# The end of the 16-head attention: each mix of the last pair waits for its own chunk and writes its own PSUM bank, and the last chunk is inverted in two halves

## The reference

```python
x = x + jnp.tanh(g_xattn[0]) * _L0_xattn_ref(ctx_1024, mask_BxS2_bf1, _layernorm(x, axis=-1), ...)
x = x + jnp.tanh(g_ffn[0]) * _L0_ffn_ref(_layernorm(x, axis=-1), ...)
...
# in _L0_xattn_ref: HEADS = 16, DIM_HEAD = 64, 2048 queries, 1601 + 2048 keys
alphas = jax.nn.softmax(sim, axis=-1)
out = jnp.einsum('bhqf,bhfd->bhqd', alphas, v)
out = out.transpose(0, 2, 1, 3).reshape(b, q_len, INNER)
return out @ Wo
```

## Time and profile before

| | us |
|---|---|
| median of 3 runs | 3281.27 (3280.16 to 3281.69) |
| profiled execution, its own time | 3278.4 |
| its span, first to last instruction | 3276.5 |
| PE busy | 3067.5 |
| VectorE busy | 2211.0 |
| ScalarE busy | 1951.7 |
| last product with V to the last add (the part around the change) | 1800.1 to 1816.5 on the span |

### The profile page before, as it was taken

The page is one execution under the profiler, slowest core; times in us unless marked ns, Lnnn a source line. Parts: engine busy times, 40 slices in busy tenths (PEclk is TensorE's granted clock), DMA queues, the critical chain, the costliest instruction groups (busy, mean ns, idle before and its releaser), DMA issues. The chain is left out here.

```text
span 3276.5 us, 69950 instructions
## 1 busy us (share of the span) xinstructions
PE 3067.5 (94%) x29122; PEld 1640.0 (50%) x29122; DVE 2211.0 (67%) x2812; ACT 1951.7 (60%) x2424; POOL 115.6 (4%) x163
## 2 busy tenths in 40 slices
PE   6999999999999999999999788999979988999988
PEld 3444444444444444444445673222247767767767
DVE  6888887878887878788878753000057765577655
ACT  5665656656656556556556226999936653266631
POOL 0000000000000000000000100000011110021100
PEclk8999999999999999999999799999989999999989
DMA  2000000000000000000000012010120001000000
GB/s 77 7 2 2 8 2 8 2 2 8 2 2 8 2 8 2 2 3 2 2 3 2 30 44 73 27 35 27 27 70 11 11 1 57 14 7 14 1 1 26
DMA packets 30027, 51.58 MB, mean 16 GB/s; under 512 B 6071, under 2 KB 22538, under 8 KB 28554
## 3 DMA queue, kind: packets, MB, share of 16 engines
q1 hardware_dynamic: 29706, 46.91, 4.5%
HBM read 41.04 MB, written 5.83 MB: 14 GB/s over the span
## 5 line engine op out<-in xcount | busy, mean ns | idle before, releaser
L716 ACT ACTIVATE a_probs<-PS 128x1024 f32<-128x1024 f32 x928 | 949.6, 1024 | 601.8 <-PE PS L476 599.0
L489 PE MATMUL PS<-a_probs,a_V 64*64 64x512 f32 x7424 | 976.2, 590 | 5.8 <-DVE a_heads_outT L897 5.0
L930 DVE TENSOR_TENSOR a_prob_sums<-a_prob_sums,a_probs 128x1024 f32<-128x1024 f32 x512 | 627.3, 1225 | 153.3 <-ACT a_probs L716 137.9
L927 DVE SCALAR_TENSOR_TENSOR a_prob_sums<-a_probs,a_valid,a_prob_sums 128x1024 f32<-128x1024 f32 x384 | 481.1, 1253 | 70.2 <-ACT a_probs L716 60.3
L476 PE MATMUL PS<-a_Q_hi,a_K_hi 64*64 64x512 f16 x3712 | 382.2, 381 | 5.5 <-ACT a_probs L716 4.8
L1690 ACT ACTIVATE c_probs<-PS 128x1024 f32<-128x1024 f32 (+1 forms) x416 | 382.4, 1086 | 5.4 <-PE PS L1609 3.7
L476 PE MATMUL PS<-a_Q_lo,a_K_hi 64*64 64x512 f16 x3712 | 381.4, 377 | 1.9 <-issue 1.9
L476 PE MATMUL PS<-a_Q_hi,a_K_lo 64*64 64x512 f16 x3712 | 379.2, 377 | 1.0 <-issue 1.0
L489 PEld LDWEIGHTS PS<-a_probs,a_V 64*64 64x64 f32 x7424 | 287.8, 133 | 163.3 <-issue 20.8
L476 PEld LDWEIGHTS PS<-a_Q_hi,a_K_hi 64*64 64x64 f16 x3712 | 118.5, 106 | 277.4 <-issue 271.5
L476 PEld LDWEIGHTS PS<-a_Q_hi,a_K_lo 64*64 64x64 f16 x3712 | 119.0, 107 | 227.9 <-issue 225.6
(11 more groups left out here) (309 smaller groups left out, 4103.6 us busy)
## 6 DMA issues: line engine op xcount, KB each, us to landing
c_Qop<-q_part SPq DMA_DIRECT2D x96, 64.0 KB, 2.2
c_Kop<-k_part SPq DMA_DIRECT2D x96, 50.0 KB, 2.0
d_raw<-in_l1f_w_dram SPq DMA_DIRECT2D x18, 256.0 KB, 3.2
d_tables<-in_rotary_dram SPq DMA_DIRECT2D x2, 2048.0 KB, 12.6
d_wqkv<-in_l1f_wqkv_dram SPq DMA_DIRECT2D x2, 1536.0 KB, 6.4
X<-in_x_dram SPq DMA_DIRECT2D x2, 1024.0 KB, 9.6
out_dram<-X SPq DMA_DIRECT2D x4, 512.0 KB, 3.5
c_cT<-in_ctxT_dram SPq DMA_DIRECT2D x1, 1601.0 KB, 6.4
```

Source lines behind the costliest of these rows:

```text
L489: last = nc.tensor.matmul(m.PS[64 * h:64 * h + 64, PVB + g, :], V[e][rows, s, 64 * h:64 * h + 64], probs[n % 4][rows, h * BANK:(h + 1) * B ...
L716: nc.scalar.activation(probs[n % 4][:], m.PS[:, b0:b0 + 2, :].rearrange("p b c -> p (b c)"), ACT.Exp).then_inc(exped, 1)
L927: nc.vector.scalar_tensor_tensor(out=sums, in0=new, scalar=valid[:, s:s + 1], in1=sums, op0=ALU.mult, op1=ALU.add).then_inc(summed, 1)
L930: nc.vector.tensor_tensor(sums, sums, new, ALU.add).then_inc(summed, 1)
```

## The change

Three things change. In `mix`, the mixes of the last pair wait for `heads_done` to reach the value of their own chunk instead of all four chunks. The last pair's 8 mixes and adds use 8 different banks, in the order 0, 1, 2, 3, 7, 4, 5, 6, so that no mix waits for an add; the mixes in banks 4 and 6 wait until what else lies there has been read (`block_out`, `inverted`). And DVE handles the last chunk in two halves: two reciprocals, then the product for these 256 columns (`scale_half`), and the same again. `heads_done` thus counts 32 after the first half and 33 after the second. Pairs 0 to 6 keep their code.

```diff
+        LAST_MIX_BANKS = (0, 1, 2, 3, UNIT, PVB, PVB + 1, TOTAL)
...
-                    if u < 2:
+                    if i == PAIRS - 1:
+                        pe.wait_ge(heads_done, i * CHUNKS + (u // 2 + 1 if u < MIXES - 1 else CHUNKS + 1))
+                    elif u < 2:
                         pe.wait_ge(heads_done, (i + 1) * CHUNKS)
...
                 total(PAIRS - 1, CHUNKS - 1)
-                for u in range(MIXES):
-                    if u >= 4:
-                        pe.wait_ge(added, (PAIRS - 1) * MIXES + (u - 3))
-                    mix(PAIRS - 1, u, u % 4)
+
+                for u, bank in enumerate(LAST_MIX_BANKS):
+                    if bank == PVB:
+                        pe.wait_ge(block_out, PAIRS * CHUNKS)
+                    if bank == TOTAL:
+                        pe.wait_ge(inverted, PAIRS * CHUNKS * PARTS)
+                    mix(PAIRS - 1, u, bank)
...
+                def scale_half(j):
+
+                    part = slice(j * 2 * P, (j + 1) * 2 * P)
+                    dve.wait_ge(inverted, (PAIRS * CHUNKS - 1) * PARTS + 2 * (j + 1))
+                    dve.wait_ge(block_out, PAIRS * CHUNKS)
+                    heads = heads_outT[:, (CHUNKS - 1) * BANK:CHUNKS * BANK][:, part]
+                    nc.vector.tensor_tensor(heads, heads, inverse[:, part], ALU.mult).then_inc(heads_done, 1)
...
-                for j in range(PARTS + 1):
-                    invert(PAIRS - 1, CHUNKS - 1, j)
-                for u in range(MIXES):
-                    add(PAIRS - 1, u, u % 4)
+
+                for half_chunk in range(2):
+                    for j in (2 * half_chunk, 2 * half_chunk + 1):
+                        invert(PAIRS - 1, CHUNKS - 1, j)
+                    scale_half(half_chunk)
+                for u, bank in enumerate(LAST_MIX_BANKS):
+                    add(PAIRS - 1, u, bank)
```

## The result

| | before | changed |
|---|---|---|
| median of 22 runs each, us | 3283.44 (3277.71 to 3287.64) | 3277.75 (3273.11 to 3280.88) |
| ratio of the runs, 95% interval | | 0.9981 (0.9974 to 0.9987) |
| profiled execution, its own time | 3278.4 | 3279.85 |
| last total's first matmul to the next block's first statistics | 16.75 | 11.29 |

The ratio is worth 3283.44 x 0.0019 = 6.2 us, and its interval 4.3 to 8.5. The forecast was a gain of 5.3 us, 0.16%, for the median. It lies in that interval, and the measured median, 3277.75, lies in the forecast range. The interval of the ratio doesn't reach 1, so the gain is real, and it is just under the 0.2% line.

A forecast was written before the change was run, and what follows sets the result against it. PE, busy 94%, bounds most of the span; reciprocals and product, mixes, then one add set the pair's end. 5.5 us off the median 3281.27 gave 3275.8; a quarter microsecond less gain gave 3276.0, range 3273.9 to 3278.8.

The forecast's parts named there:

- The order of the mixes and DVE's pace: End of last pair: mixes start behind the total at 0.86 us each; DVE's adds, 0.65 us apart, then set the pace.
- The halves: DVE's last chunk: second half product ends 0.23 us later than the whole one; the early first half gains nothing.
- The check by pieces: End of last pair: 4.5 us idle and some 5 us low clock leave the chain, adds take back 4.5.
- the main sum: End of last pair: last add ends at 1811.0 instead of 1816.50, a gain of 5.5 us.
- The banks: Last pair's mixes: banks 0 to 3 and 7 are free, bank 4 is read before PE gets there.
- I take off a quarter of a microsecond for this: Mixes of before: low clock cost 2.9 us in the profile, perhaps less in other executions; gain lowered by a quarter microsecond.
- Rival (b): Mixes of before: most executions lose little to the clock; gain 0.5 to 4.3 us, 2.5 with no fall; chance 0.19.
- What PE loses there has up to 2.3 us of cover: Next block: PE's losses to the clock are covered by its 2.32 us wait for DVE's L60.
- the term put at nothing: Next block: clock rises and falls up to 1852.5 need not move by the same 5.5 us; costed at nothing.

The follow-up runs named there:

- the one with GpSimd later: Changed kernel without halves, four double-width adds, the first moved to ScalarE and GpSimd, GpSimd waiting for the last chunk's product: stretch 9.90 us, ratio 0.9987 to before.

## Why the prediction was right

**The order of the mixes and DVE's pace: right, to 0.1 us.** Counted from the total's start, the first half product was to be at 3.14 us and is at 3.14, the second at 5.26 and is at 5.27, the first add at 5.59 and is at 5.62, the end of the adds at 10.9 and is at 10.97. The half product takes 0.42 us. The adds take 5.35 us for 8; the rule of the Trainium skill ("VectorE: DVE Perf Modes", "The DRAIN you can't avoid") that I had set against the row would have given 6.0. I had quoted it without its exception, which the same section states: a next operation that is not held starts earlier. What holds an instruction is in the page's section "Two Vector instructions with no wait between them". The trace agrees with the exception.

**The halves: right.** Forecast as a loss of 0.23 us, measured as 0.25 both ways: in the stretch when taken from the changed kernel, and in the start of the mixes when added to before.

**The check by pieces: wrong, though it came out at 5.5.** "4.5 us of PE's idle time and some 5 us of low clock go out of the chain" has both pieces wrong. The pause doesn't leave the chain, since DVE's reciprocals and product, which fill it, set the end in both kernels. And by the prediction's own figure the low clock was 2.9 us, not 5. What leaves is the way from the last product's end over the mixes to the last add's end, 1816.50 - 1805.53 = 10.97 us. What takes its place is 5.35 us of adds and 0.25 for the halves, less the 0.09 by which the first add starts before the product has ended, together 5.51. 10.97 - 5.51 = 5.46 us is the gain between the two profiles, and the main sum had these terms right.

**The banks: not said clearly enough.** I credited the early mixes and the eight banks together. The runs split them: the banks taken out change nothing (11.29), the banks alone leave the pause of 4.52 us, and the halves are a small loss. So the waits for the own chunk are the whole gain. No run has these waits alone; the one without the banks still has the halves, which cost 0.25.

**The term that was mis-sized is the clock of the mixes of before.** The step "I take off a quarter of a microsecond for this" was too small, and no row had given its size. The stretch of before is 16.75 us in the profile that I worked from, and 15.54, 16.19 and 15.64 - 0.25 = 15.39 in three others that have the same pause and chain: on average 16.0. Without any low clock it is 13.86. So the clock's part was 2.9 us in the first profile and 2.1 on average, 0.8 less and not 0.25, and the gain of the stretch is on average 16.0 - 11.3 = 4.7 us, not 5.5. Four profiles are few for an average. The last three were also taken on three different chips, so that a difference between chips isn't excluded; on these three the changed kernel, or one with the same order of work at this end, stayed at 11.29 to 11.30. Rival (b) had the right mechanism and was never complete: none of these four shows the mixes at the full clock from their start.

The measured median is 1.7 us above the forecast 3276.0, and that is the base, not the change: the forecast stood on 3281.27, the median of three runs, and over 22 runs that of before is 3283.44, 2.2 us more. The gain by the medians is 5.7 us where 5.3 was forecast. That this didn't leave the range, whose upper end is 3278.8, is in part luck.

**"What PE loses there has up to 2.3 us of cover" was wrong.** The time from the next block's statistics to its down product was 46.2 us in three profiles (the first of before, the changed kernel with 8 additional matmuls, the one with GpSimd later), 47.7 to 48.0 in four and 48.3 in six; the run with 20 matmuls is left out. In the six of 48.3 us the clock stayed low until some 24 us behind the first statistics. The second profile of the changed kernel is one of them (timeline of DVE; L1130 are the outer products on PE, L1264 the update of the weights with them):

```profile
1830.98 0.75 DVE L1264 SCALAR_TENSOR_TENSOR b_W1T<-PS,b_scale,b_W1T 128x512 f32<-128x512 f32 x1 [0.69 <-PE PS L1130]
...
1833.51 1.55 DVE L1264 SCALAR_TENSOR_TENSOR b_W1T<-PS,b_scale,b_W1T 128x512 f32<-128x512 f32 x2
1836.02 0.75 DVE L1264 SCALAR_TENSOR_TENSOR b_W1T<-PS,b_scale,b_W1T 128x512 f32<-128x512 f32 x1 [0.96 <-PE PS L1130]
```

```profile
1817.00:1841.00 24.00, 15.81 (x44) 10.54 (x45) 21.74 (x54) 5.52 (x9) 2.88 (x3) 0.51 0.28 100
```

The outer products took 7.19 us there, and DVE waited for them, 0.69 and 0.96 us. In the first profile of before the clock was full for most of their time, and they took 4.14:

```profile
1828.89 4.14 PE L1112 MATMUL PS<-b_blocks,b_pairs 8*128 8x512 f32 x8
...
1832.88 2.06 DVE L1246 SCALAR_TENSOR_TENSOR b_W1T<-PS,b_scale,b_W1T 128x512 f32<-128x512 f32 x3
```

The last of these updates ends 20.25 us behind the first statistics in the one and 18.11 in the other. That is 2.14 us, the whole difference between 48.32 and 46.19. PE's wait of 2.3 us for L60, which I took for cover, is still there in the second profile of before (2.29 us), whose time is 48.34: DVE's work, for which PE waits there, was late by the same 2.1 us, so the wait covered nothing. Where the four profiles of 47.7 to 48.0 lose theirs was not followed up.

This is no effect of the change as far as the profiles tell. It strikes both kinds of kernel: 46.19, 48.34, 48.34 and 48.33 us with the pause of before, and from 46.17 to 48.35, also 47.8 on average, in the seven with early mixes and nothing added to the next block. So the term put at nothing was nothing in the sum, by balance between the two kernels and not by cover.

**Why two profiles of whole runs mislead.** The part ahead of the last total took between 1800.08 and 1806.39 us in 14 profiles with the same work up to there, and the first exponential was at 73.1 us in the first profile of before and at 76.2 in that of the changed kernel. So 3.1 of the 5.6 us between these two had come about by then. In the first 60 us their mean clock differs, 0.91 and 0.83. That the clock's falls at other moments make the whole of these 6 us is argued, not shown. It is as large as the gain, and the first profile of before had the shortest of all 14.

What is left open: the ratio says 6.2 us (4.3 to 8.5), the stretches 4.7 on average, from 4.1 (15.39 - 11.29) to 5.5. Both fit, and nothing more precise can be had from the times.

## What to carry to other kernels

Give a wait the value of what its instruction really reads; here the wait values of six mixes made the gain, because PE had these six ready while it waited for a chunk that they don't use. Ask then which engine has all the work that is left, since only its instructions count from there: the halves and the banks served PE, which no longer set the end. And measure an edit of a few microseconds in its own stretch and in more than one profile, since the same pause ahead of the mixes cost 1.5 to 2.9 us of clock in four profiles.

## What the runs showed of the hardware

- A pause of PE of 4.5 us cost the products behind it 1.5 to 2.9 us more by the clock, in four executions of the same chain. Nine unread matmuls in the pause took this to nothing (13.86 us for the stretch).
- Outer products of the next block took 7.19 us while the clock was at 0.50 and 4.14 where it was full for most of them, and DVE's updates, which wait for them, ended 2.1 us later.
- A product on DVE with both operands in SBUF took 2.52 us instead of 0.69 beside a GpSimd add; adds with one operand in PSUM kept 1.25 us beside the same add.
- Matmuls of 128x512 with fp32 operands took 7.10 us for 8 at the full clock, 0.89 us each, and not the 0.43 that I had reckoned from one record of the two.
